# A two-layer graph network on one core: adding the high and the low halves of every neighbour sum in TensorE's accumulator instead of on VectorE

## The reference

```python
def _layer(x, rows, cols, vals, W, b):                 # twice, W0/b0 then W1/b1
    neigh = jax.ops.segment_sum(vals[:, None] * x[cols], rows, num_segments=N)   # vals = 1 / degree of rows
    return jax.nn.relu(jnp.concatenate([x, neigh], axis=1) @ W.T + b)
...
    h_self, h_neigh = feat @ W_self, feat @ W_neigh
    h_sparse = _maxk(h_neigh, 32)                      # the 32 largest of each row, the rest 0
    summed = jax.ops.segment_sum(h_sparse[src], dst, num_segments=n)
    return h_self + summed / jnp.maximum(deg, 1.0)[:, None]
...
x = _layernorm(x + L0(x, src, dst, ...))               # two layers
x = _layernorm(x + L1(x, src, dst, ...))               # the last stage
```

## Time and profile before

| what | value |
|---|---|
| time, median of 3 runs | 682.12 us |
| lowest and highest | 681.74, 683.88 us |
| the profiled execution's own time | 683.04 us |
| its span, first to last instruction | 681.2 us |
| PE busy, PEld busy | 647.5 us (95%), 337.0 us (49%) |
| DVE busy, ACT busy, POOL busy | 497.7 (73%), 338.3 (50%), 107.7 (16%) us |
| mean granted TensorE clock | 0.981 of full |

### The profile page before, as it was taken

The page is one execution under the profiler, slowest core; times in us unless marked ns, Lnnn a source line. Parts: engine busy times, 40 slices in busy tenths (PEclk is TensorE's granted clock), DMA queues, the critical chain, the costliest instruction groups (busy, mean ns, idle before and its releaser), DMA issues.

```text
span 681.2 us, 11240 instructions
## 1 busy us (share of the span) xinstructions
PE 647.5 (95%) x3966; PEld 337.0 (49%) x3967; DVE 497.7 (73%) x1274; ACT 338.3 (50%) x654; POOL 107.7 (16%) x187
## 2 busy tenths in 40 slices
PE   8768989999978999999999999999999999999996
PEld 4455657667534444444444444444444444444442
DVE  8886979999777888788883487878878855643333
ACT  3656979999776676767773233333333320000000
POOL 3001222222111101110010322223232210000000
PEclk9977999999998999999999999999999999999999
DMA  8423555555521111010112556465555523310000
GB/s 214 103 88 108 191 170 186 165 162 176 158 69 38 36 34 44 32 45 31 42 35 65 161 158 189 149 188 155 176 167 171 144 79 116 116 32 23 26 28 23
DMA packets 39543, 73.09 MB, mean 107 GB/s; under 512 B 3120, under 2 KB 32207, under 8 KB 39481
## 3 DMA queue, kind: packets, MB, share of 16 engines
q1 hardware_dynamic: 39481, 72.30, 35.3%
HBM read 38.91 MB, written 33.38 MB: 106 GB/s over the span
## 4 chain that ended last, share of the span: by engine, by line
PE 85%; DVE 7%; ACT 3%; DMA 2%; issue 2%; SPq 0%; POOL 0%; DVEq 0%; POOLq 0%; ACTq 0%
PE pair L1557 37%; PE bank L1669 10%; PE pair L1669 10%; PE bank L1481 6%; PE bank L1455 5%; PE bank L1447 5%; PE pair L1455 4%; PE pair L1367 4%; PE bank L1461 2%; DVE hots L637 2%; DMA own_in<-own_dram 1%; DMA wparts_dram<-w_parts 1%; PE pair L1346 1%; PE bank L1467 1%; ACT a L1226 1%
## 5 line engine op out<-in xcount | busy, mean ns | idle before, releaser
L1557 PE MATMUL pair<-xs,ct 125*128 125x512 f16 x625 | 143.0, 380 | 0.0
L1557 PE MATMUL pair<-a,ct 125*128 125x512 f16 x625 | 142.8, 379 | 0.0
L637 DVE TENSOR_TENSOR hots<-iota,jobs 125x1792 f16<-125x1792 f16 (+1 forms) x100 | 103.3, 1067 | 3.9 <-PE pair L1367 3.3
L1557 PEld LDWEIGHTS pair<-xs,ct 125*128 125x128 f16 x625 | 61.1, 100 | 68.2 <-issue 0.8
L1557 PEld LDWEIGHTS pair<-a,ct 125*128 125x128 f16 x625 | 61.1, 99 | 68.1
L1068 ACT ACTIVATE slab<-pair 125x875 f16<-125x875 f32 (+1 forms) x100 | 83.2, 855 | 11.2 <-PE pair L1367 6.8
L1226 ACT ACTIVATE a<-ct 125x1000 f16<-125x1000 f16 (+1 forms) x75 | 80.2, 1069 | 8.3 <-DMA c_dram<-slab 7.4
L1669 PE MATMUL bank<-xs,ct 125*128 125x512 f16 (+1 forms) x325 | 71.5, 379 | 0.0
L1669 PE MATMUL pair<-xs,ct 125*128 125x512 f16 x300 | 66.4, 379 | 0.0
L529 POOL TENSOR_TENSOR own_in<-own_in,bias_sb 125x256 f32<-125x256 f32 x50 | 38.3, 767 | 168.1 <-DMA own_in<-own_dram 167.9
L1301 ACT ACTIVATE sd<-mv,epsb 125x1 f32<-125x1 f32 x25 | 7.4, 294 | 113.9 <-DVE mv L1004 113.9
(11 more groups left out here) (205 smaller groups left out, 821.6 us busy)
## 6 DMA issues: line engine op xcount, KB each, us to landing
c_dram<-slab SPq DMA_DIRECT2D x25, 683.6 KB
ct<-c_dram SPq DMA_DIRECT2D x25, 683.6 KB
own_in<-own_dram SPq DMA_DIRECT2D x50, 125.0 KB
own_dram<-own SPq DMA_DIRECT2D x25, 125.0 KB
own_dram<-own_st SPq DMA_DIRECT2D x25, 125.0 KB
x_in<-in_x_dram SPq DMA_DIRECT2D x25, 125.0 KB
z_dram<-z_st SPq DMA_DIRECT2D x25, 125.0 KB
a<-z_dram SPq DMA_DIRECT2D x5, 625.0 KB
```

Of the source, the lines that this page charges most:

```text
L637: v.tensor_tensor(hots[k][:, :, :, :].rearrange("p w g (a d) -> p (w g) a d", d=2), iota, job, ALU.is_equal).then_inc(win_hot, 1)
L1557: ins = mm(agg[k % 3][0:lhs.shape[1], :], lhs, parts[l][:, t, :], start=t == 0, stop=t == NT - 1, skip_group_check=True)
```

## The change

In `aggregate` and in `last_sum` the one matmul of 512 columns per block becomes two matmuls of 256 columns with the same stationary block: the first takes the high columns of the features, the second the low ones, and both add into columns 0 to 256 of the same bank. The bank then holds the sum of both halves. On VectorE `first_half` and `second_half` become one `mean`, and L1001 goes; the waits that stood between the halves go with them. Line numbers behind L905 are lower by 6 to 9 in the kernel after.

```diff
-            def first_half(l, T):
+            def mean(l, T):
                 k = l * NT + T
                 dve.wait_ge(own_biased, k + 1)
                 dve.wait_ge(deg_ready, T + 1)
                 dve.wait_ge(agg_done, k + 1)
-                return noted(v.scalar_tensor_tensor(t2[k % 2][:, :], agg[k % 3][0:P, 0:F], rdeg[l][:, T:T + 1],
-                                                      own_in[k % 2][:, :], ALU.mult, ALU.add))
-
-            def second_half(l, T):
-                k = l * NT + T
-                v.scalar_tensor_tensor(t2[k % 2][:, :], agg[k % 3][0:P, F:2 * F], rdeg[l][:, T:T + 1], t2[k % 2][:, :],
-                                       ALU.mult, ALU.add).then_inc(t2_ready, 1)
+                v.scalar_tensor_tensor(t2[k % 2][:, :], agg[k % 3][0:P, 0:F], rdeg[l][:, T:T + 1],
+                                       own_in[k % 2][:, :], ALU.mult, ALU.add).then_inc(t2_ready, 1)
...
             for T in range(NT):
-                dve.wait_ge(dve_step, first_half(0, T))
-                second_half(0, T)
+                mean(0, T)
...
-                half = first_half(1, T)
+                mean(1, T)
                 if K >= 0:
                     largest(K, 0)
-                dve.wait_ge(dve_step, half)
-                second_half(1, T)
                 if K >= 0:
                     replace(K, 0)
...
-                step(v.scalar_tensor_tensor(z, ps[0:P, 0:F], rdeg_dst[:, T:T + 1], z, ALU.mult, ALU.add))
-                v.scalar_tensor_tensor(z, ps[0:P, F:2 * F], rdeg_dst[:, T:T + 1], z, ALU.mult, ALU.add).then_inc(n3_read, 1)
+                v.scalar_tensor_tensor(z, ps[0:P, 0:F], rdeg_dst[:, T:T + 1], z, ALU.mult, ALU.add).then_inc(n3_read, 1)
...
-                    ins = mm(agg[k % 3][0:lhs.shape[1], :], lhs, parts[l][:, t, :], start=t == 0, stop=t == NT - 1,
-                             skip_group_check=True)
+                    for pt in range(2):
+                        ins = mm(agg[k % 3][0:lhs.shape[1], 0:F], lhs, parts[l][:, t, pt * F:pt * F + F],
+                                 start=t == 0 and pt == 0, stop=t == NT - 1 and pt == 1, skip_group_check=True)
...
-                    ins = mm(out3[T % 8][0:lhs.shape[1], :], lhs, xs[:, b, :], start=b == 0, stop=b == NT - 1,
-                             skip_group_check=True)
+                    for pt in range(2):
+                        ins = mm(out3[T % 8][0:lhs.shape[1], 0:F], lhs, xs[:, b, pt * F:pt * F + F],
+                                 start=b == 0 and pt == 0, stop=b == NT - 1 and pt == 1, skip_group_check=True)
```

## The result

The kernel after takes 691.8 us (median of 4 runs, 690.49 to 692.94), the kernel before 683.0 us beside it (median of 4, 681.74 to 683.88): ratio 1.0106, 95% interval 1.0072 to 1.014 (the ratios, here and below, are estimates over all runs and not quotients of the two medians, which would be 1.0129 here).

What follows compares the result with a forecast made beforehand. PE was taken to bound the kernel: 4.76 us of added matmul cost less VectorE gains of 0.52, 0.52 and 0.48 us gives +3.2 us, taking the median from 682.12 to 685.3 us, range 683.2 to 688.5.

Steps and rivals of the forecast that it cites:

- The supply of instructions is not short either: PE's sums: 21.0 instructions per us seen from 95 to 180 us, against 18.3 needed afterwards, so no loss.
- The clock: Rival at the start of layer 0: a shorter first wait might keep PE's clock up, +1.7 us, 683.8 us; chance 0.10.
- The prediction's own sign of being wrong: In the layers: prediction is wrong if PE's idle time hasn't gone down by about 1 us.
- The fixed cost: Each matmul in the sums: 2.54 ns beyond its columns, 218.42 ns a pair, 4.76 us over 1875 blocks.
- Neither bound, 0 nor 3.8: Limits on the added cost per block in the sums: nothing to 3.8 ns, 0 to 7.1 us over all blocks.
- The tail: Behind the last matmul: one VectorE operation less, 0.52 us gained.
- the join at the start of layer 0: PE's 1.11 us wait at 197.89 gets shorter by one VectorE operation: 0.52 us gained.
- The start of layer 1: PE's 0.48 us wait at 380.93 disappears, as its chain gets 0.52 us shorter: 0.48 us gained.
- No cost for same columns: Rival in the sums: adding twice as often into the same columns costs 2 x 163 ns per block, 600 us; chance 0.08 together with unhidden loads.
- no exposed loads: Rival in the sums: added weight loads don't hide, up to 98 ns each, 184 us; chance 0.08 together with same-column writes.

Runs made afterwards that it cites:

- e9: Kernel before with the split made only for the first two sums of layer 0 (50 of 1875 blocks): 689.7 us, ratio 1.0068.
- e4: Kernel after with the first two sums of layer 0 back to whole 512-column matmuls and their joins on VectorE: 690.63 us, ratio 1.0085.
- e6: Kernel before with 100 never-run matmuls added to the general case, so the layers' code lies as in after: 685.51 us, ratio 1.0022.
- e5: Kernel after, unchanged, measured again against the kernel before: 690.29 us, ratio 1.0101.
- e7: Kernel after, but the two 256-column matmuls go into two halves of the bank and VectorE joins as before: 691.81 us, ratio 1.013.
- e3: Kernel after with 28 never-run matmuls (56 instructions) added to the general case, moving only the layers' code: 690.67 us, ratio 1.0101.
- e1: Kernel after with PE's never-run general-case code left out, so no taken jump into the layers: 686.85 us, ratio 1.0046.
- e8: Kernel before with only the last sum in four 128-column matmuls per block, into four quarters of the bank: 688.63 us, ratio 1.0064.
- e10: Kernel before with the change made in the last stage alone: 685.17 us, ratio 1.002.
- e2: Kernel before with PE's never-run general-case code left out, as control: 686.32 us, ratio 1.0029.
- e11: Kernel before with the change only at T = 0 of each layer and the last T of the last stage (75 blocks): 683.52 us, ratio 0.9985.

## Why the prediction was wrong

- **"The supply of instructions is not short either" failed.** I compared a mean rate, 21.0 instructions per us over 85 us of straight code, with the 18.3 needed, and by that rate the supply is enough, as layer 1 and the last sum show at that rate without a wait. But PE's program jumps once where the stages that change begin, and there it isn't the rate that counts but how long the queued matmuls last against a fetch of 2.4 to 2.9 us (3.5 once, in e9). Before, the fetch came in just in time. From the packet's appearance PE had 3.0 to 3.1 us of matmuls left in three profiles with whole matmuls (before, e4, e6), and with halves 1.1 to 1.2 us in four (after, e5, e7, e9) and 0.65 us in e3. That the jump is the cause is shown by e1 (no jump, no wait), e4 (cover back, no wait) and e9 (cover gone for 50 blocks alone, both waits); that the second wait is the end of a packet, by e3 and e6, which move it by code that never runs. e1 takes out the test of the edge count along with the jump, so the two aren't told apart by e1 alone; that a fetch by itself stops PE for as long is shown by the second wait in e6, with no branch in between. Price: 3.4 us between the medians of e5 and e1 (1.8 at equal clock), by profiles of layer 0 3.1 us (e5) to 5.0 us (the first profile), of which 2.0 to 2.2 are idle time (7.31 and 7.53 us against 5.31) and the rest the clock.
- **The clock** I had as a rival for a gain. It went the other way: PE's idle time there grew by 1.6 us (1.4 in e5) and the clock was at 0.83 in 195 to 225 us (0.89 in e5) instead of 0.94. The prediction's own sign of being wrong, PE's idle time in the layers not going down by 1 us, is the one that came true.
- **The fixed cost was right**: 2.5 ns per matmul at 256 columns, 218.4 ns a pair. Neither bound, 0 nor 3.8, was near. The reason given for choosing 2.54 was weaker than the result: 500 is an even count too and had 5.6 ns over, so that 256 would go with 512 and not with 500 was partly luck. With the jump taken out most of the forecast stands: e1 is 2.9 us over before, 3.1 at equal clock, for 3.2. By the stages of its profile it is 3.6 us (0.98 in layer 0, 1.58 in layer 1, 1.03 in the last sum and the tail), since the next item's gain is missing.
- **The tail was right**: 0.52 us. So was the join at the start of layer 0, once nothing else waits: 1.11 to 0.50 us in e1.
- **The start of layer 1 was sized too large.** The wait was to go from 0.48 to 0. In the profiles with the change in layer 1 it is 0.17 us (the first), 0.42 (e5), 0.50 (e1) and none (e3, e4); in those with layer 1 as before it is 0.30 (e9), 0.47 (e8), 0.48 (before, e10), 0.57 (e2) and 0.74 (e6). That is 0.3 us less on average, with a wide spread, since L901 there waits for GpSimd's L529 and that for the DMA of `own_in`. What the change does to the chain itself is steadier: from the start of L901 to the end of L545 it takes 4.39 us before, 4.39 or 4.40 in e2, e6, e8, e9 and e10, and 4.39, 4.29, 4.30, 4.30 and 4.34 us in after, e1, e3, e4 and e5. Almost nothing of the 0.52 us arrives. VectorE's and GpSimd's rows of the kernel after show why:

```profile
384.28 0.73 POOL L529 TENSOR_TENSOR own_in<-own_in,bias_sb 125x256 f32<-125x256 f32 x1 [0.36 <-DMA own_in<-own_dram]
384.61 0.69 DVE L960 SCALAR_TENSOR_TENSOR t<-t,x_in 125x256 f32<-125x256 f32 x1
...
387.45 0.43 DVE L960 SCALAR_TENSOR_TENSOR t<-t,x_in 125x256 f32<-125x256 f32 x1
387.47 0.93 POOL L545 TENSOR_TENSOR part<-t,part 125x256 f16<-125x256 f32 x1 [2.46 <-ACT part L1268]
```

  The chain, moved up by 0.52 us, now meets the other engine twice: L960 takes 0.69 us beside L529, where its like at 387.45 takes 0.43, and L545 takes 0.93 us beside VectorE instead of 0.67. Together that gives 0.52 us back. e11 bears it out in part: it drops the join of T = 0 alone and keeps that of T = 1, `y_low` (L548 there) takes 0.67 us again, and the chain takes 4.03 us. That it is the overlap is read from these rows; no run was made to test it by itself.
- **No cost for same columns, no exposed loads**: both rivals were rightly small (e7; PEld 5842 at 218.4 ns a pair).

What stays open: how much the lost clock costs on average, and so the price of the jump between 1.8 and 5.0 us. It differs from run to run, and the profiles here are one execution each.

## What to carry to other kernels

Before cutting matmuls into smaller ones, look for jumps in PE's program: what hid the fetch behind a taken branch here was some 29 queued instructions, and with matmuls of half the length 12 to 22 were left, which lasted 0.65 to 1.2 us instead of 3.0. A wait put down to "issue" beside a packet on the instruction queue is its sign. On an engine that bounds the kernel count instructions as well as columns: here 2.5 ns each outweighed every operation saved on an engine with time to spare, and the saving pays only where the bound engine waits for it. Where runs scatter, compare at equal clock too and read stages in the trace; neither the medians nor the equal clock alone would have settled this case.

## What the runs showed of the hardware

- A matmul has a fixed 2.5 to 2.6 ns at full clock at 128, 256 and 512 columns (e8, after, before). At 500 and 125 columns it was 5.6 and 3.5 ns, which remains unexplained.
- The first instruction behind a jump, or behind the end of a fetched packet there, comes 2.4 to 2.9 us after its packet is seen (3.5 us once, in e9), and code that never runs can move such a wait by its length alone (e3, e6).
- A short idle time can cost as much again by the clock: in e9, 2.16 us more idle came with a clock of 0.89 instead of 0.94 over 30 us, an estimated 1.5 us. It need not: in e6, with 0.4 us more idle and a single wait of 2.76 us, and in e3 the clock stayed at 0.94.
- A two-input fp32 operation took 0.58 to 0.69 us on VectorE beside one of GpSimd's where it takes 0.43 us otherwise, and GpSimd's took 0.93 instead of 0.67 us (after, e1, e3, e4, e5).
